# 32 zero products in place of 48 at the start, the down weights behind the out weights, and new orders for five engines

## What is computed

```python
xn = _layernorm(x)                                   # x: (4, 512, 256)
q, k, v = xn @ Wq.T, xn @ Wk.T, xn @ Wv.T            # 16 heads of 16
w = softmax(q @ k.T / 4 + causal mask)
s = (w @ v) @ Wo.T
W = (wq - 128) * scale[:, None]                      # gate, up, down
g = silu((silu(xn @ Wgate.T) * (xn @ Wup.T)) @ Wdown.T)
out = x + s * g
```

## Time and profile before

| | us |
|---|---|
| median of 3 runs | 302.65 (302.5 to 303.17) |
| the profiled execution | 303.55 |
| its span, first to last instruction | 301.8 |
| TensorE busy | 282.9 (94%) |
| VectorE busy | 209.6 (69%) |
| ScalarE busy | 175.1 (58%) |
| GpSimd busy | 134.8 (45%) |
| mean granted clock of TensorE | 0.981 |

### The profile page before, as it was taken

One profiled execution on the slowest core, in us unless ns is written; L12 is line 12 of the kernel. 1 busy time (PEld: TensorE's weight loads), 2 busy tenths in 40 slices (PEclk: granted clock), 3 DMA queues, 4 the chain that ended last, 5 costly groups with the idle time before them and its releaser, 6 DMA issues.

```text
span 301.8 us, 6042 instructions
## 1 busy us (share of the span) xinstructions
PE 282.9 (94%) x2134; PEld 209.5 (69%) x2134; DVE 209.6 (69%) x722; ACT 175.1 (58%) x260; POOL 134.8 (45%) x234
## 2 busy tenths in 40 slices
...
GB/s 269 179 0 58 176 225 139 164 197 102 182 62 160 68 0 4 1 5 147 181 255 150 114 70 3 3 14 208 213 128 129 87 74 2 2 2 4 139 2 70
DMA packets 20529, 30.09 MB, mean 100 GB/s; under 512 B 2308, under 2 KB 10116, under 8 KB 20500
## 3 DMA queue, kind: packets, MB, share of 16 engines
...
...
## 4 chain that ended last, share of the span: by engine, by line
PE 60%; DVE 22%; ACT 7%; issue 4%; POOL 4%; DMA 2%; SPq 1%; ACTq 0%; DVEq 0%; POOLq 0%
DVE ps L1117 12%; PE ps L426 12%; PE ps L428 10%; PE ps L427 10%; PE ps L620 7%; PE ps L604 6%; PE ps L475 5%; PE ps L581 4%; ACT pt L870 3%; DVE mx L1117 2%; DMA qk_scratch<-hid 2%; PE ps L670 2%; DVE hh L1098 1%; DVE hid L1091 1%; DVE wol L1233 1%
## 5 line engine op out<-in xcount | busy, mean ns | idle before, releaser
L1117 DVE CUSTOM_DVE_ANT_0 ps<-ps,later 128x512 f32<-128x512 f32 (+3 forms) x256 | 117.0, 527 | 16.3 <-PE ps L581 16.3
L870 ACT ACTIVATE pt<-ps 128x1024 f32<-128x1024 f32 x80 | 78.4, 1030 | 9.7 <-PE ps L604 9.6
L986 POOL TENSOR_SCALAR_AFFINE_SELECT pt<-pt 128x256 f32<-128x256 f32 (+1 forms) x112 | 47.3, 439 | 74.9 <-ACT pt L870 73.9
L957 POOL TENSOR_TENSOR hid<-hid 128x512 f32<-128x512 f32 (+1 forms) x24 | 30.8, 1288 | 38.5 <-DVE hid L1091 27.8
L426 PE MATMUL ps<-xh,guh 128*128 128x512 f32 x88 | 38.1, 433 | 0.6 <-DVE hid L1091 0.3
L581 PE MATMUL ps<-kp,qp 48*128 48x512 f32 (+3 forms) x256 | 31.5, 346 | 6.0 <-DVE mx L1117 5.9
L1117 DVE DVE_READ_ACCUMULATOR2_ANT mx<- 128x1 f32 x256 | 36.7, 143 | 0.0
L620 PE MATMUL ps<-pt,vt 128*17 128x512 f32 (+3 forms) x480 | 35.2, 434 | 0.4 <-POOL pt L986 0.3
L604 PE MATMUL ps<-qp,kp 50*128 50x512 f32 (+3 forms) x256 | 33.2, 351 | 2.0 <-DVE mx L1117 1.3
L428 PE MATMUL ps<-xh,gul 128*128 128x512 f32 x88 | 34.8, 395 | 0.0
L427 PE MATMUL ps<-xl,guh 128*128 128x512 f32 x88 | 34.8, 395 | 0.0
...
## 6 DMA issues: line engine op xcount, KB each, us to landing
...
```

Source lines behind the costliest of these rows:

```text
L870: nc.scalar.activation(pt[:, at:at + 2, :], ps[:, base:base + 2, :], ACT.Exp, scale=SCALE).then_inc(exp_done, 1)
L957: nc.gpsimd.tensor_tensor(a, a, hid[part, m % 2, 1, :], ALU.mult).then_inc(h_done, 1)
L986: mm = nc.gpsimd.affine_select(out=diag, in_=diag, compare_op=ALU.is_ge, fill=0.0, base=0, pattern=[[0, diag.shape[1]], [1, P]], channel_m ...
L1117: mm = nc.vector.tensor_tensor_reduce(part, part, later[:, T - w:], -1.0, HUGE, ALU.add, ALU.min, mx[:, n % 2, to:to + 1])
```

## The change

The wait on wol in front of wds, 32 zero products for 48, a wait on xl in front of qk0.1 (which now comes ahead of qd0.1), and new texts for all five engines and for the banks. The units themselves, their number and their instructions stay. Of the texts, the lines on which the steps below rest:

```diff
@@ TENSOR @@
-t0.0@0 t0.1@1 qd0.0@2 qd0.1@3 qk0.1@4 qd0.2@5 qd0.3@6 qk0.2@7 qk0.3@0 m0.0@2 m0.1@4 m0.2@6 gu0.0@1 gu0.1@2
-gu0.2@3 m0.3@4 m0.4@6 gu0.3@2 gu0.4@0 gu0.5@1 c0.0@4 gu0.6@5 m0.5@6 m0.6@2 m0.7@0 gu0.7@4 gu0.8@6 gu0.9@7
-gu0.10@2 m0.8@0 m0.9@4 v0.0@3 v0.1@6 t1.0@7 t1.1@3 s0.0@0 c0.1@2 s0.1@4 s0.2@6 qk1.0@3 s0.3@0 m0.10@4 qk1.1@2
-s0.4@6 m0.11@0 m0.12@4 qk1.2@3 pv0.0@2 m0.13@6 m0.14@0 m0.15@4 m0.16@6 m0.17@0 m0.18@4 c0.2@6 qk1.3@7 gu1.0@3
...
+t0.0@0 t0.1@1 qd0.0@2 qk0.1@3 qd0.1@4 qk0.2@5 qd0.2@6 qd0.3@7 qk0.3@0 m0.0@2 m0.1@4 m0.2@6 gu0.0@1 gu0.1@2
+gu0.2@3 m0.3@4 m0.4@6 gu0.3@2 gu0.4@1 gu0.5@0 c0.0@4 gu0.6@5 gu0.7@4 gu0.8@2 gu0.9@3 m0.5@6 m0.6@0 m0.7@4
+gu0.10@2 m0.8@6 v0.0@3 m0.9@0 v0.1@4 t1.0@5 t1.1@2 s0.0@6 s0.1@0 c0.1@3 s0.2@6 s0.3@4 qk1.0@2 qk1.1@3 m0.10@0
+s0.4@6 qk1.2@2 s0.5@4 pv0.0@3 s0.6@6 s0.7@0 s0.8@4 s0.9@6 m0.11@0 m0.12@4 m0.13@0 m0.14@6 m0.15@4 m0.16@0
+m0.17@6 m0.18@4 c0.2@2 qk1.3@2 gu1.0@0 gu1.1@1 m0.19@6 gu1.2@4 zt0.0@5 pv0.1@2 c0.3@3 dn0.0@5 zt0.1@6 dn0.1
+z0.0@7 dn0.2@6 s0.10@2 s0.11@0 dn0.3 s0.12@2 m1.0@0 gu1.3@5 m1.1@6 m1.2@2 m1.3@0 gu1.4@5 m1.4@6 gu1.5@4 m1.5@2
+s0.13@0 gu1.6@4 s0.14@6 s0.15@0 m1.6@2 c1.0@5 gu1.7@6 gu1.8@7 pv0.2@6 s0.16@0 s0.17@4 s0.18@2 zt0.2@7 gu1.9@6
+s0.19@0 s1.0@4 gu1.10@7 m1.7@2 m1.8@0 pv0.3@6 s1.1@4 s1.2@2 v1.0@7 zt0.3@6 s1.3@0 m1.9@4 m1.10@2 z0.1@6 v1.1@7
+m1.11@0 m1.12@4 s1.4@2 c1.1@0 m1.13@2 t2.0@1 t2.1@0 m1.14@6 m1.15@4 dn1.0@1 qk2.0@0 qk2.1@2 qk2.2@3 c1.2@0
...
+s3.12@6 m3.17@4 m3.18@2 s3.13@0 s3.14@4 m3.19@6 zt3.1@2 gu3.8@3 gu3.9@2 c3.3@0 gu3.10@1 pv3.2@0 o2.0@1 s3.15@6
@@ SCALAR @@
-woh0.0 qhi1.2 ccp0.2 qhi1.3 wdh0.0 exp0.5 zcp0.0 exp0.6 exp0.7 tanh1.0 exp0.8 up1.0 fth0.0 exp0.9 exp0.10 fth0.1
+exp0.5 woh0.0 exp0.6 exp0.7 exp0.8 exp0.9 qhi1.2 ccp0.2 wdh0.0 qhi1.3 zcp0.0 zcp0.1 tanh1.0 ccp0.3 up1.0 fth0.0
@@ VECTOR @@
-gate0.4 max0.8 max0.9 gate0.5 shift0.1 xlo1.0 xlo1.1 hst0.0 max0.10 qlo1.0 qlo1.1 max0.11 max0.12 wol0.0 max0.13
-max0.14 max0.15 shift0.2 max0.16 qlo1.2 max0.17 max0.18 qlo1.3 wdl0.0 norm0.0 gate1.0 u0.0 u0.1 gate1.1 norm0.1
+qdl0.3 max0.0 max0.1 max0.2 gate0.0 qlo0.3 max0.3 max0.4 gate0.1 shift0.0 gate0.2 gate0.3 gate0.4 max0.5 max0.6
+max0.7 gate0.5 max0.8 max0.9 hst0.0 shift0.1 xlo1.0 xlo1.1 qlo1.0 max0.10 qlo1.1 wol0.0 max0.11 max0.12 max0.13
+max0.14 max0.15 shift0.2 qlo1.2 max0.16 max0.17 max0.18 wdl0.0 qlo1.3 max0.19 norm0.0 shift0.3 gate1.0 norm0.1
+u0.0 zlo0.0 u0.1 max1.0 gate1.1 max1.1 max1.2 max1.3 max1.4 max1.5 shift1.0 gate1.2 gate1.3 max1.6 gate1.4 bn2.0
@@ GPSIMD @@
-mask0.0 mask0.1 mask0.2 mask0.3 mask0.4 wds0.0 wdc0.0 mask0.5 mask0.6 mask0.7 mask0.8 hid1.0 mask0.9 mask0.10
+mask0.0 mask0.1 mask0.2 mask0.3 mask0.4 mask0.5 mask0.6 mask0.7 mask0.8 mask0.9 wds0.0 wdc0.0 hid1.0 mask0.10
@@ build @@
             pe.wait_ge(cn_zero, 1)
-            warm(48)
+            warm(32)
...
                 bank = take("qk", b, c)
-                if b and c == 0:
+                if c == (0 if b else 1):
                     pe.wait_ge(xlo_done, KD * (b + 1))
...
             def shift_d(b, _):
                 pool.wait_ge(wd_loaded, 64)
+                pool.wait_ge(wol_done, 1)
```

More of the change, by code:

```diff
@@ L45 @@
[L45 to L59, removed]
@@ new lines @@
+m1.11@0 m1.12@4 s1.4@2 c1.1@0 m1.13@2 t2.0@1 t2.1@0 m1.14@6 m1.15@4 dn1.0@1 qk2.0@0 qk2.1@2 qk2.2@3 c1.2@0
+s1.5@6 pv1.0@2 s1.6@4 s1.7@6 dn1.1 dn1.2@0 zt1.0@2 s1.8@4 s1.9@6 qk2.3@1 dn1.3 s1.10@2 m1.16@4 m1.17@6 o0.0@1
+m1.18@2 m1.19@4 pv1.1@0 s1.11@6 o0.1@1 zt1.1@0 s1.12@2 s1.13@6 s1.14@4 c1.3@1 z1.0@0 gu2.0@2 gu2.1@3 m2.0@6
+m2.1@0 m2.2@4 gu2.2@3 m2.3@6 gu2.3@2 gu2.4@0 gu2.5@1 gu2.6@4 m2.4@6 m2.5@2 m2.6@0 pv1.2@5 s1.15@6 s1.16@2
+gu2.7@4 s1.17@6 s1.18@0 s1.19@2 zt1.2@5 c2.0@4 m2.7@6 gu2.8@5 m2.8@0 m2.9@2 m2.10@6 gu2.9@4 gu2.10@0 s2.0@2
@@ new lines @@
+m2.11@4 pv1.3@1 c2.1@6 m2.12@2 v2.0@7 v2.1@6 zt1.3@7 t3.0@4 t3.1@5 m2.13@2 m2.14@0 s2.1@6 z1.1@4 s2.2@6 s2.3@2
+qk3.0@5 s2.4@6 s2.5@2 m2.15@0 qk3.1@4 c2.2@5 qk3.2@6 m2.16@2 m2.17@0 m2.18@4 pv2.0@7 m2.19@2 s2.6@0 o1.0@7
+s2.7@4 s2.8@0 s2.9@2 zt2.0@6 c2.3@4 o1.1@5 s2.10@0 dn2.0@4 pv2.1@5 s2.11@6 s2.12@2 s2.13@0 zt2.1@5 dn2.1 z2.0@5
+dn2.2@6 dn2.3 s2.14@2 s2.15@0 qk3.3@7 m3.0@4 m3.1@2 m3.2@0 pv2.2@6 s2.16@4 m3.3@2 zt2.2@6 gu3.0@0 m3.4@4 s2.17@6
+gu3.1@1 s2.18@2 s2.19@6 m3.5@4 gu3.2@1 c3.0@0 m3.6@2 m3.7@4 m3.8@6 gu3.3@0 pv2.3@2 s3.0@4 s3.1@6 s3.2@0 m3.9@2
@@ new lines @@
+v3.0@4 zt2.3@5 c3.1@6 v3.1@7 z2.1@6 s3.3@2 s3.4@0 m3.10@4 gu3.4@7 s3.5@2 m3.11@0 m3.12@4 gu3.5@6 m3.13@2 m3.14@0
+pv3.0@6 s3.6@4 s3.7@2 s3.8@0 zt3.0@6 gu3.6@7 c3.2@6 s3.9@4 m3.15@2 m3.16@0 gu3.7@6 pv3.1@4 s3.10@2 s3.11@0
+s3.12@6 m3.17@4 m3.18@2 s3.13@0 s3.14@4 m3.19@6 zt3.1@2 gu3.8@3 gu3.9@2 c3.3@0 gu3.10@1 pv3.2@0 o2.0@1 s3.15@6
+s3.16@4 s3.17@2 dn3.0@0 s3.18@6 s3.19@4 dn3.1 pva3.3@1 o2.1@2 z3.0@3 zt3.2@0 pvb3.3@6 pvc3.3 oa3.0@4 ztb3.3@7
+zta3.3@6 oa3.1@0 za3.1@6 dn3.2@2 zb3.1@3 o3.0 dn3.3 o3.1
@@ L70 @@
[L70 to L79, removed]
@@ new lines @@
+exp0.5 woh0.0 exp0.6 exp0.7 exp0.8 exp0.9 qhi1.2 ccp0.2 wdh0.0 qhi1.3 zcp0.0 zcp0.1 tanh1.0 ccp0.3 up1.0 fth0.0
+zhi0.0 exp0.10 exp0.11 fth0.1 exp0.12 hhi1.0 tanh1.1 up1.1 hhi1.1 tanh1.2 up1.2 exp0.13 tanh1.3 exp0.14 exp0.15
+ccp1.0 hhi1.2 up1.3 tanh1.4 hhi1.3 zcp0.2 exp0.16 exp0.17 exp0.18 up1.4 exp0.19 exp1.0 tanh1.5 up1.5 zcp0.3
+exp1.1 exp1.2 hhi1.4 vcp1.0 exp1.3 hhi1.5 zhi0.1 xn2.0 xn2.1 xn2.2 exp1.4 xn2.3 vcp1.1 ccp1.1 xhi2.0 xhi2.1
+qhi2.0 qhi2.1 ccp1.2 exp1.5 zcp1.0 exp1.6 exp1.7 fth1.0 qhi2.2 exp1.8 exp1.9 qhi2.3 fth1.1 exp1.10 zcp1.1
```

70 lines of the change are left out of this document (35 added, 35 removed).

## The result

The changed kernel takes **311.26 us** (median of 3 runs, 309.88 to 311.65), the kernel before 302.65: a ratio of 1.028 (95% interval 1.024 to 1.032). It is slower, on the side of the forecast of 308.6 and inside its range. The profiled execution took 311.65 us, its span 309.9; of before these were 303.55 and 301.8, so the traces stand 8.1 us apart.

A forecast was written before the change was run, and what follows sets the result against it. TensorE's own work was taken as the floor, with only its waits to win or lose. Terms -3.0 - 2.55 + 2.45 + 11.2 - 2.2 = +5.9 gave 308.6 us for the median, 8-in-10 range 300.0 to 312.5.

The forecast's parts named there:

- The head, -3.0: At the start: sixteen zero products less let the first projection begin at 14.39 us, a gain of 3.0 us.
- The gap of "0.7 us": TensorE idles 0.7 us ahead of the first projection, covered by nothing but short.
- A rise as late as the rival's: At the start: clock rises only behind the 64th pass, +1.7 us, 310.3 us; chance 0.02.
- The out weights, -2.55: First batch: VectorE's rest of the out weights runs free of GpSimd's shift of the down weights, gaining 2.55 us.
- shift0.2, +2.45: Ahead of c0.2: its second instruction is held by GpSimd's product of the down weights, costing 2.45 us; bounds 0 and 3.4.
- The orders, +11.2, less 2.2: Whole kernel: new orders force 21.9 us of TensorE idle time against 10.7, +11.2; late starts that no longer count return 2.2.
- eight small stretches: Eight smaller places where the new orders make TensorE wait, 0.2 to 1.0 us each, 4.6 us together.
- the clock, "no difference": In front of c0.2: the clock should fall again as before, no difference, bounds -2.3 and +2.3 us.
- Idle time above 20 us: Sign that the forecast is right: TensorE idle above 20 us, most of it put to VectorE.
- Faster: Rival at s0.6 to c0.2: maxima start early, shift0.2 passes free, the clock stays up; 300.3 us, chance 0.15.
- No change: Rival behind 80 us: 8 us, not 2.2, is taken back because other waits end together; 302.7 us, chance 0.08.
- The second fall near dn1.0: Rival around zt0.3 to dn1.0: the clock falls a second time, costing 5 us, 313.5 us; chance 0.10.

The follow-up runs named there:

- the gap filled: Kernel before with 32 zero products at the start in place of 48, and 14 in place of 6 behind the first batch's transposes: 300.15 us, ratio 0.992.
- the kernel with the head alone: Kernel before with 32 zero products at the start in place of 48, nothing else: 301.38 us, ratio 0.994.
- the wait: Kernel before with GpSimd's shift of the down weights waiting for VectorE's rest of the out weights, nothing else: 303.52 us, ratio 1.002.
- late out weights: Kernel before with VectorE's rest of the out weights moved from behind max0.12 to behind qlo1.2: 302.12 us, ratio 0.998.
- the last experiment: Kernel before with 32 and 14 zero products, out weights behind qlo1.2, and the down weights' product waiting for shift0.2: 299.31 us, ratio 0.990.
- the kernel with 48 products: Changed kernel with 48 zero products again in place of 32, its orders and added wait kept: 312.87 us, ratio 1.029.
- the cheaper maxima: Both kernels with maxima reading half of each block's columns (at least 128) and a smaller exponential scale: 296.58 us in orders of before, 299.01 in those of after.

## Why the prediction was right, and where it was not

*The head, -3.0.* Right in the profile: 14.41 against 14.39. Its working had an error that did not matter there: the transposes began at 10.67, not 11.19, for the clock rose earlier; xl of VectorE set the start, as said. Over the experiments the transposes behind 32 products began between 9.88 and 11.23. This is the difference from run to run that the Trainium skill states in "TensorE: Matmul & The Clock Gate", Part 1, and the trace agrees. The size of 3.0 is in part the luck of one trace: of five kernels with 48 products the first projection began between 15.95 and 17.36, and the trace of before is the latest. Against 15.95 it would be 1.5; by the medians it is 2.2 with the gap filled. The gap of "0.7 us" was 1.36 in after and 2.06 in the kernel with the head alone, where the clock fell right behind it, at 14.67. That cost was not in the sum. A rise as late as the rival's was not seen in any trace.

*The out weights, -2.55.* Right: 0.69 us. The added wait ended nothing late.

*shift0.2, +2.45.* Right in place and size, a copy of 2.42 us beside the product of the down weights, and c0.2 waited behind it for 2.3; wrong in the instruction. The step said that the subtraction with two SBUF inputs is held because it has two. Held was the copy in front of it, with one, in after and in six of the experiments' traces, for 1.15 to 3.20 us; the subtraction took 0.17 to 0.32 each time. The Trainium skill, in "SBUF — State Buffer", section "Who interferes with whom", names copies and casts too among VectorE's instructions that can take the ports shared with GpSimd, and says that the one that issues second is fully blocked. The traces agree: the copy ended 0.02 to 0.04 us behind GpSimd's product in after (75.11 and 75.08) and in the kernels with the wait and with the late out weights. Two SBUF inputs are held as well, as the out weights' 2.38 us in the last experiment and the earlier trace rows show. In the earlier trace rows, however, the out weights ended at 64.73, 0.34 us ahead of the shift's end at 65.07, so there the hold did not last to the end.

*The orders, +11.2, less 2.2.* Without the head, the sum of the terms is -2.55 + 2.45 + 11.2 - 2.2 = 8.9; the distance measured is 11.1. dn0.0 is 7.6 us later than in before, but s0.8, s0.9, m0.19, pv0.1 and c0.3, some 3.3 us of TensorE, now stand ahead of it; so it is 4.3 late by the same work, where the sum gave +1.8 (-3.0 - 2.55 + 2.45 + 4.9). The other 3.8 of the 8.1 come behind it, where the sum gave 6.3 - 2.2 = 4.1. (Ahead of dn0.0 the prediction has 10.1 in the new order and 5.2 in the old; with its eight small stretches all behind, that leaves 11.8 and 5.5 there.)

Behind dn0.0 the number is near, but the mechanism isn't seen. The count is of idle time, and from dn0.0 to the end TensorE is idle for 11.6 us in after and 10.9 in before: 0.7 more. The rest is busy time, and two falls of the clock lie in it, with 3.4 us of lost work, which the sum put at zero. It may be that TensorE at half clock works through time in which it would have waited. But two runs of the kernel with 48 products speak against that: from 0.972 to 0.961 the mean clock loses some 7 us more at half clock (an estimate, twice the difference of the shortfalls times the spans), and the time grew by 2.7 us, most of the 3.5 that half clock costs with TensorE full. By that rate some 2.6 of the 3.8 us are the clock's and about 1 the orders'. So the agreement here is in part luck. That VectorE's maxima are the cause of half to two thirds of the loss is shown by the cheaper maxima.

*The term that was mis-sized: the clock, "no difference".* The low stretches took 9.3 us of TensorE's work in after and 3.5 in before, 5.8 more where the sum put nothing. Ahead of dn0.0, where 2.5 us are missing from the sum, one part is seen: the clock fell at 53.8, ahead of the stretch that the argument was about, while TensorE had work throughout (3.40 of 3.40). That is 1.7 us, and pv0.0 started at 60.19 in place of 57.9, c0.2 at 75.98 in place of 71 to 74. The other is that the fall at 67.4 lasted 13.6 us in place of ten and took 4.2 us of work in place of 3.5; how much of that counted is not settled, since TensorE waits for VectorE in much of it. In this stretch "no difference" nearly holds: it has a low clock in both kernels. With the clock at 5.8 in place of zero and only 2.2 us missing from the whole, the orders' own term was probably too large, and the two errors partly cancel; what waits absorbed of the clock's loss is not known exactly.

*Idle time above 20 us.* Wrong: 16.9, 4.1 more than in before; behind 85 us it is 6.9, close to the 6 us that the prediction named as a sign against its count. Idle and lengthened busy time together are 11 us more than in before, which is the measured loss.

*The rivals.* Faster needed m0.11 by 60; it started at 65.01. No change needed other waits to absorb 8 us; the measured loss is larger than the sum, so nothing of that size was absorbed. The second fall near dn1.0 came, at 132.3, where the rival had it, and lasted 3.4 us in place of ten, 1.7 at most in place of 5. The bounds of the clock, 2.3 either way, just hold the excess: +2.2 in place of zero gives 310.8 for the median, 311.26 measured.
